# Adding beta to the residual rows on GpSimd in a two-layer attention and feed-forward kernel, and storing the last tile in halves

## The reference

```python
x = x + attn(layernorm(x))                      # x1, 4096 rows of 1024
h = layernorm(x1)
shared = relu(h @ up_w) ** 2 @ down_w           # 1024 -> 2048 -> 1024
routed = (h @ fc1_w @ expert_w * sum(top2(h @ gate_w))) @ fc2_w
y = shared + routed
out = x1 + (y - mean(y)) * rsqrt(var(y) + 1e-5) * gamma + beta
```

## Time and profile before

| | us |
|---|---|
| median of 3 runs | 2267.76 |
| the profiled execution | 2281.12 |
| its span, first to last instruction | 2279.3 |
| PE busy | 2219.4 (97%) |
| DVE busy | 1478.0 (65%) |
| ACT busy | 609.6 (27%) |
| POOL busy | 542.6 (24%) |

### The profile page before, as it was taken

The page is one execution under the profiler, slowest core; times in us unless marked ns, Lnnn a source line. Parts: engine busy times, 40 slices in busy tenths (PEclk is TensorE's granted clock), DMA queues, the critical chain, the costliest instruction groups (busy, mean ns, idle before and its releaser), DMA issues.

```text
span 2279.3 us, 36554 instructions
## 1 busy us (share of the span) xinstructions
PE 2219.4 (97%) x15001; PEld 1424.1 (62%) x15001; DVE 1478.0 (65%) x1851; ACT 609.6 (27%) x950; POOL 542.6 (24%) x464
## 2 busy tenths in 40 slices
PE   6989999999999999999999999999999999999998
PEld 5646566666665444486487478458548747846853
DVE  7756467778886699776476376466556546637615
ACT  4323334334422574232012012102202201211200
POOL 2322100000002488352034024104203302311400
PEclk9989999999999999999999999999999999999999
DMA  9999478999996889878767966966876877795672
GB/s 233 195 168 212 84 148 213 233 233 226 204 201 165 277 294 304 266 260 252 230 217 221 273 206 207 292 203 206 275 215 207 232 243 226 210 303 172 204 229 85
DMA packets 510951, 502.75 MB, mean 221 GB/s; under 512 B 330816, under 2 KB 351424, under 8 KB 510784
## 3 DMA queue, kind: packets, MB, share of 16 engines
q1 hardware_dynamic: 501040, 470.00, 74.4%
q10 hardware_dynamic: 8880, 27.27, 4.3%
q0 software_dynamic: 864, 3.15, 0.4%
HBM read 351.44 MB, written 69.73 MB: 185 GB/s over the span
## 4 chain that ended last, share of the span: by engine, by line
PE 66%; DVE 19%; ACT 5%; DMA 3%; issue 3%; SPq 2%; POOL 0%; ACTq 0%; DVEq 0%; POOLq 0%
PE psum L97 43%; PE psum L2078 22%; ACT arena L840 4%; DVE b_mx L948 3%; DVE arena L983 3%; DVE arena L1288 2%; DVE arena L1272 2%; DVE arena L974 1%; DVE arena L992 1%; DMA arena<-arena 1%; SPq L1334 1%; DVE a_stats L474 1%; DMA arena<-in_attn_Wqkv 0%; DVE arena L979 0%; DMA arena<-in_ffn_up_w 0%
## 5 line engine op out<-in xcount | busy, mean ns | idle before, releaser
L97 PE MATMUL psum<-arena 128*128 128x256 f16 (+1 forms) x11592 | 1609.1, 302 | 29.0 <-DMA arena<-arena 13.1
L97 PEld LDWEIGHTS psum<-arena 128*128 128x128 f16 x11592 | 1134.8, 98 | 498.7 <-issue 33.7
L2078 PE MATMUL psum<-arena 128*128 128x512 f16 x2352 | 509.9, 379 | 0.0
L2078 PEld LDWEIGHTS psum<-arena 128*128 128x128 f16 x2352 | 230.1, 98 | 276.0
L1526 POOL TENSOR_TENSOR arena<-arena 128x256 f32<-128x256 f32 x70 | 95.6, 1366 | 433.7 <-ACT arena L1652 433.7
L840 ACT ACTIVATE arena<-psum,b_nb,consts 128x512 f32<-128x512 f32 x128 | 97.9, 774 | 232.5 <-DVE b_nb L952 232.5
L1795 DVE TENSOR_TENSOR arena<-arena 128x1536 f16<-128x1536 f32 (+1 forms) x28 | 59.0, 2106 | 122.4 <-ACT arena L1576 121.4
L1581 ACT ACTIVATE c_ystd<-c_ymv,c_epsc,consts 128x1 f32<-128x1 f32 x32 | 12.4, 387 | 412.2 <-DVE c_ymv L1817 412.2
L1513 POOL TENSOR_TENSOR arena<-arena 128x256 f32<-128x256 f32 x56 | 41.8, 747 | 283.4 <-DVE arena L1905 283.4
L1635 ACT ACTIVATE arena<-arena 128x768 f16<-128x768 f32 x56 | 47.2, 843 | 230.0 <-DVE arena L1905 230.0
L324 POOL TENSOR_TENSOR arena<-arena 128x1024 f16<-128x1024 f32 x30 | 64.3, 2144 | 178.0 <-ACT arena L357 178.0
(11 more groups left out here) (160 smaller groups left out, 1794.0 us busy)
## 6 DMA issues: line engine op xcount, KB each, us to landing
arena<-ws_in SPq DMA_DIRECT2D x210, 512.0 KB, 3.8
arena<-ws_out SPq DMA_DIRECT2D x196, 512.0 KB, 4.7
arena<-in_attn_x SPq DMA_DIRECT2D x64, 512.0 KB, 5.0
arena<-x SPq DMA_DIRECT2D x64, 512.0 KB, 6.5
arena<-ws_in SPq DMA_DIRECT2D x70, 256.0 KB, 3.7
x<-arena SPq DMA_DIRECT2D x32, 512.0 KB, 4.0
out<-arena SPq DMA_DIRECT2D x32, 512.0 KB, 6.2
ws_in<-arena SPq DMA_DIRECT2D x30, 512.0 KB, 4.3
```

The lines of the kernel that those rows point to most:

```text
L97: last = nc.tensor.matmul(out, lhs(a, c), rhs(b, c), start=(c == 0 and n == 0), stop=(c == chunks - 1 and n == len(PRODUCTS) - 1))
L2078: mm = nc.tensor.matmul(product_banks(m)[:, u, :], rS[:, c, a, LEFT[m], u * P:(u + 1) * P], w2[slot_of(i, n)][:, cc, b, :], start=(c == 0 ...
```

## The change

POOL gets a new step, `residual_sum`: as soon as a tile's x1 rows are in their buffer it adds beta to them, in place. DVE's pass over 1/std then adds this sum, and the pass that added the x1 rows is gone. POOL needs beta, so its `first_body` now begins with the wait for `gb_in`. In the last tile of the last block that DVE pass is done in two halves of 512 columns, each followed by a store of its own.

```diff
@@ sync_program
-        for t in range(2, TILES):
-            store(NBLK - 1, t)
-        for t in range(TILES):
-            hold(out_sent[t], 16 * (NBLK + 1))
+        store(NBLK - 1, 2)
+        t = r_order(NBLK - 1)[TILES - 1]
+        for h in range(2):
+            cols = slice(h * BANK, (h + 1) * BANK)
+            hold(out_ready, TILES * NBLK + 2 + h)
+            sync.dma_start(out_d[NBLK - 1, t][:, cols], acc[:, t, cols]).then_inc(out_sent[t], 16)
+        for n in range(TILES):
+            hold(out_sent[n], 16 * (NBLK + 1 + (n == t)))
@@ pool_program
+        def residual_sum(i, q):
+            pool.wait_ge(xres_in[q % 2], 16 * (2 * i + q // 2 + 1))
+            pool.tensor_tensor(xres[q % 2], xres[q % 2], beta, ALU.add).then_inc(xres_summed, 1)
+
         def first_body():
+            pool.wait_ge(gb_in, 32)
             for p in range(FIRST_PAIRS):
                 pair_sums(p)
...
             pool.wait_ge(unit_lo, 2 * IN_TIME)
             for s in range(UNIT_SEMS):
                 pool.wait_ge(unit_out[s], units_out(s, 2 * IN_TIME))
+            for q in range(TILES):
+                residual_sum(0, q)
@@ body(i, last) of pool_program
             if not last:
                 for q in range(2):
                     differences(i + 1, q)
+            for q in range(TILES):
+                residual_sum(i, q)
@@ routed of dve_program
-                steps.link(dve.scalar_tensor_tensor(row, row, yrstd[:], beta, ALU.mult, ALU.add))
-                dve.wait_ge(xres_in[q % 2], 16 * (2 * i + q // 2 + 1))
-                dve.tensor_tensor(row, row, xres[q % 2], ALU.add).then_inc(out_ready, 1)
+                dve.wait_ge(xres_summed, TILES * i + q + 1)
+                for h in range(2 if last and q == TILES - 1 else 1):
+                    cols = slice(h * BANK, (h + 1) * BANK) if last and q == TILES - 1 else slice(0, H)
+                    dve.scalar_tensor_tensor(row[:, cols], row[:, cols], yrstd[:], xres[q % 2][:, cols], ALU.mult, ALU.add
+                                             ).then_inc(out_ready, 1)
```

More of the change, by code:

```diff
@@ L1157, in mixture @@
     xres_in = [sem(f"xres_in{s}") for s in range(2)]
+    xres_summed = sem("xres_summed")
     out_sent = [sem(f"out_sent{t}") for t in range(TILES)]
@@ L1691, in act_program @@
         turns(body)
-    NORM, NORM_S, ROUTE, OUT = 4, 3, 1 + TILES + 1, 5
+    NORM, NORM_S, ROUTE, OUT = 4, 3, 1 + TILES + 1, 4
     BEFORE = 2
```

## The result

The changed kernel takes **2280.84 us** (median of 20 runs, 2271.44 to 2285.55), the kernel before 2270.01 us (20 runs, 2265.06 to 2276.31) on the same chips: ratio **1.0046, 95% interval [1.0038, 1.0055]**, 10.4 us slower. The forecast was 2274.2 us, 6.4 us slower, with a range up to 2280. The sign and the lag behind gamma and beta came out as forecast; the time lies 0.8 us outside the range. By the bound of 0.5% it is the case "within", to which the forecast gave 0.87.

What follows compares the result with a forecast made beforehand. It took DVE's chain through block 0, from beta's load to the sixth L1812, to set the end, with PE busy afterwards. Terms 8.0 + 3.3 - 2.4 - 2.5 = 6.4 us on 2267.8 gave 2274.2 us, range 2264 to 2280.

Steps and rivals of the forecast that it cites:

- the case "within": Whole kernel: the time changes by no more than 0.5% either way; chance 0.87.
- Part 1: Head of POOL's program: waiting for gamma and beta moves eight adds beside DVE in block 0, 8.0 us later.
- tile 34's split: Sign in block 0: the split comes some 8 us later; less than 4 us late would show the forecast wrong.
- the lag is absorbed: Rival, block 0: idle gaps of DVE and POOL take up the eight adds, -2.6 us, 2265 us; chance 0.17.
- no meeting at the end of block 0: Rival, end of block 0: POOL's new adds meet only DVE's PSUM passes, 3.1 us slower, 2270.9 us; chance 0.12.
- part 3: POOL's new adds: at block 0's end they hold up DVE's two-input passes, 3.3 us, ends 0 and 4.2.
- The two counted meetings: End of block 0, tile 0: POOL's adds delay DVE's L1821 by 1.5 us and L1824 by 3.3 in all.
- Parts 2 and 3: End of block 0: two passes taken from DVE gain 2.4 us; POOL's new adds meeting DVE cost 3.3 us.
- Part 4: After PE's end: a pass less in tile 2 and halves in tile 3 save 2.5 us, ends 1.3 and 3.0.
- PE's clock: Block 0, tile 6: a longer PE wait lowers its clock, and PE would lose some 2.5 us.
- PE's lag at the end of block 0: End of block 0: PE comes out some 7 us late, DVE's chain 8.0 late and ending the wait.
- the third rival: Block 0: ACT becomes the late one in the first three rounds, lag 11 to 13 us, 2280 us; chance 0.11.

Runs made afterwards that it cites:

- kernel 1: The changed kernel with POOL's wait for gamma and beta moved behind its pair sums, just ahead of the first residual sum: 2271.77 us, ratio 1.0001.
- kernel 2: The kernel before with only POOL's wait for gamma and beta added ahead of its first pair sum: 2281.72 us, ratio 1.0045.
- kernel 8: The changed kernel, head wait kept, with block 0's residual sums of tiles 1 to 3 each held until the tile before is out: 2274.29 us, ratio 1.0016.
- kernel 6: The kernel before with only the last tile's final add and its store done in two halves: 2269.53 us, ratio 1.0.
- kernel 5: The kernel before with POOL's wait for gamma and beta put between the sums of pair 0 and pair 1: 2277.13 us, ratio 1.0018.
- kernel 4: Kernel 1 with block 0's residual sums of tiles 1 to 3 each held until the tile before is out: 2267.60 us, ratio 0.9991.

## Why the prediction was right in kind and short in size

**Right.** The chain through gamma, pair 0 and DVE sets the end, POOL's wait at its head feeds eight adds into it, and nothing in block 0 absorbs them. Kernels 1 and 2 show it from both sides: the loss goes with the wait and comes with the wait. Part 1 was priced at 8.0 us and cost 8.4 in the changed kernel and 8.7 alone; L1289 came at 9.78 us after gamma (9.7 forecast), tile 34's split 8.1 us late (8 forecast). The rival "the lag is absorbed" fell: the gap of 1.40 us ahead of tile 34 is still there after the change, and POOL's idle time per pair was spent in the first three rounds, each at 1.07 us of DVE's. The rival "no meeting at the end of block 0" fell with the rows of 2.71 and 3.05 us. In blocks 1 to 7 a pass less on DVE and one more on POOL changed nothing (-0.1 us, within the 0.6 between profiles), as forecast.

The Trainium skill's page "SBUF — State Buffer", section "Who interferes with whom", calls the port pair that DVE and GpSimd share an exclusive lock, and says "Issue order, not op shape, decides who blocks." The trace agrees for passes with two inputs, in both directions: 0.35 us ahead, POOL's add took 2.35 us and DVE's pass 3.07; 0.15 us behind, it took 3.34 and the pass 1.28.

**The step that failed** is part 3, "L1824 begins at 950.0, 3.3 us late in all. (...) I take 3.3; the ends are 0 (no meeting) and 4.2 (both adds in full)". It counted two adds, because the first two loads are there in time, and stopped at tile 0. The sixth L1812, the one that its own chain named, belongs to tile 2, and between tile 0 and that reading stand two passes of tile 1. The load of tile 2's rows landed 4.7 and 3.8 us after tile 0 was out in the two profiles of the changed kernel, 5.2 in kernel 1; tile 1 needs 5.1 us from its first reading to L1841 (954.10 to 959.21). So the third add comes as tile 1's last passes run: 1.8 us more. The two counted meetings came out right (1.4 and 1.8 us measured, 3.2 together, against 3.3), in part by luck: an add takes 2.35 us and not 2.1, but the pass held up by it ends 1.08 us behind it and not a whole 1.28, and the two errors nearly cancel. The upper bound of 4.2 was no bound: it left out an add. Further 0.35 us are an idle time ahead of tile 1's aggregate, below. Parts 2 and 3 together: +0.9 forecast, +2.8 measured (5.0 for three meetings, 0.35 idle, less 2.5 for two passes gone), and kernels 1 and 8 show the cause by taking meetings away (-1.8 and -3.5 us).

**Terms that were mis-sized.** Part 1 by 0.4 us. Part 4: 3.0 us and not 2.5, since the half store brings 0.5 (kernel 6) where I took 0. PE's clock: around a wait of 2.96 us at tile 6, which ended at 774.15, the granted clock was 0.50 from 773.5 to 776.5; over ten microseconds it was 0.84 and 0.82, which by these two rows is 0.16 and 0.18 of 5 us, 1.7 in all, part of it while PE still waited (2.5 forecast). The forecast had read the row of before as a wait of 1.45 us without effect on the clock; that is the length of the row, and PE's wait in it was 0.97. PE's lag at the end of block 0 was forecast at some 7 us and was 8.7 to 10.3, still not the later one. The median lies at the price of the third rival (2280), but not by its mechanism: DVE waited for ACT in one round and not in three, and the lag was 8.4 us and not 11 to 13.

Summed: 0.4 + 1.9 - 0.5 = 1.8 us more than forecast, which is what the aligned marks show (8.15 against 6.4). That is 1.8 of the 4.4 us by which the difference of the medians was missed; the rest stays open.

**What stays open.** The timed difference is 10.4 us [8.6, 12.5], the aligned one 8.15. Of the 2.3 us between them 0.5 lie outside the interval. In the two profiles they don't lie behind the scaling of gamma, where all marks are accounted for, so they would stand in the attention phase ahead of it, where POOL no longer adds. With the loads of gamma and beta in their old place, the scaling began at 754.4 us in the mean of the four profiles without POOL's adds there, and at 753.8 in the mean of the seven with all eight of them; with over 12 us of variation between profiles this neither shows 2 us nor excludes them. The run of kernel 2, with the same head wait, has the same gap (10.2 against 8.3), kernel 8 has none (3.6 against 4.0). Chance isn't excluded, nor is a small cost there.

## What to carry over

Where a moved operation takes a new input, look where the wait for that input lands in its engine's program: one wait put at the head instead of before its first user cost 8 us here, and moving it gave them back. When two engines exclude each other for whole instructions, follow the moved instructions up to the very event that ends the critical wait, with the landing time of each one's input, and not only over the first tile. And compare profiles from a common event: the spans of these two kernels differed by 1.8 us where the kernels differed by over 8.

## What the runs showed of the hardware

- Which of two excluding instructions pays is decided by tenths of a microsecond, and can flip between a kernel and its variant (0.35 us ahead, 0.15 us behind). A DVE pass of 1.28 us behind an add of 1024 columns took 2.70 to 3.16 us at the end of block 0.
- With both engines adding without a break, POOL's adds of 512 columns (1.26 us alone) take 2.12 to 2.25 us and DVE's passes of 1024 columns 2.2 to 2.3. In the records from 769 to 809 us of the changed kernel one add ends in each pass and one pass in each add: they alternate, one and one.
- In kernel 5 even the scaling of gamma, which reads one tile of rows, took 1.85 us and not 0.75 when an add began 0.04 us after it (the add took 1.26). In the changed kernel the add began 0.06 us after it, and there the add was the longer one, 1.81 us, and the scaling took 0.75. So at such distances the order of the records doesn't tell who is held up:

```profile
759.71 1.85 DVE L1778 TENSOR_SCALAR arena<-arena,consts 128x1024 f32<-128x1024 f32 x1 [16.45 <-DMA arena<-in_ffn_ln_beta]
```

- In every kernel with the residual sums on POOL, DVE idles 0.50 us ahead of tile 1's aggregate in block 0, where it is 0.14 before and ahead of all other such aggregates, so 0.35 us more; also where no sum runs beside it (kernel 4, at 943.77). The records name only DVE's own statistics pass. Not explained.
- Two adds of 1024 columns back to back took 5.64 us beside DVE's passes (at 947.46) and 4.64 in block 1 (at 1095.03).
